# A decoder kernel's attention with heads of eight: heads regrouped by 32 rows, scores issued two units at a time, values once per step

## The chip, the cores and the metric

The kernel runs as one program on 1 core of one Trainium2 chip. The metric is the device time of that core in microseconds (us). The engines are named as the profile names them: PE (TensorE), PEld (its weight loads), DVE (VectorE), ACT (ScalarE), POOL (GpSimd), SP (SyncE). A matrix product reads its stationary operand (the "weights") and its moving operand from SBUF and writes one of eight PSUM banks.

## The reference

Sixteen sequences of 128 tokens, 128 wide, pass through a decoder of four blocks. Each block is self attention, cross attention to a context and a feed-forward part, each followed by a residual sum and a layer norm. What matters here are the five attention layers with 16 heads of 8 columns each:

```python
Q = q_in @ Wq + bq                     # (b, 128, 128) -> 16 heads of 8
scores = einsum('bhqd,bhkd->bhqk', Q, K) / sqrt(8)
scores = causal or windowed or no mask; L1_attn adds a relative bias
attn = softmax(scores)                 # over 128 keys
out = einsum('bhqk,bhkd->bhqd', attn, V) -> (b, 128, 128) @ Wo (+ bo)
```

They are L0_xattn (causal, `h8`), L1_attn (relative bias in windows of 64, `h8p`), L1_xattn (no mask, `h8`), L2_attn and L3_attn (causal, with rotary turning of queries and keys, `h8r`). All values are float32, except the causal mask, which is added by a bfloat16 product.

## The kernel before

`run_loop` is called twice: loop A holds eight layers (L0_attn to L2_xattn, without L2_ffn), loop C the last three. Each runs two iterations over 8 of the 16 sequences. A **step** is one layer on one sequence; a step is split into **units** (`UNITS`): an attention layer with heads of eight has 4 units of 4 heads. So there are 4 layers x 8 sequences x 2 iterations = 64 such steps in loop A and 16 in loop C, 80 steps or 320 units in all. All units of a loop stand in one list, and `plan.slots()` counts through it. In slot n each engine issues, in an order that is written in the code and the same for every slot:

- PE: `scores(n + 3)` (L768), `second(n)` (L821: four 128x128 transposes of the probabilities into the one `second_bank`), `values(n - 1)` (L854), then output and turn of a finished step (L892, L901) and projections of later steps (`project`, L705).
- DVE: `front(n + 3)` (L1154: the negated row maximum; in L1_attn first the bias is added, L1169), `inverse(n + 2)` (L1191), `back(n)` (L1198: copy of `second_bank` to `probs_t`), then residual and statistics (L1233), `normalise` (L1257), and takes of projections (`take`, L1082).
- ACT: `turned(n)` (L1021: the same copy, for the units in `PT_ACT`: unit 3 in `h8`, 2 in `h8p`, 1 and 3 in `h8r`), `outs(n - 1)` (L1034, L1036), `front(n + 3)` (L997, L995: exponentials of 4 heads with their sums), then takes.
- POOL: `probabilities(n + 2)` (L1358: times the inverse sums), and `spread(s)` (L1336) once per step.

Every engine works through its list strictly in order; semaphores hold it where an input is late. There are three score banks; `scores(n)` waits until the unit that used its bank three units earlier has been read (`exp_done`, or `moved` in L1_attn).

How 4 heads share one product: unit i takes heads i, i+4, i+8, i+12. POOL spreads the queries into `Qg`, where copy i holds only rows with (row mod 32) div 8 = i, scaled. The keys stand in `Km` as a block-diagonal matrix, 128 rows by 4 x 128 columns, whose block j holds rows 32j to 32j+31. One product of 128 rows gives the unit's four heads:

```python
mm = pe.matmul(bank[:, :], Qg[:, ring, i, :], Km[:, ring, :, :])            # L803, 128x512
for j in range(4):                                                          # L878, each unit
    mm = pe.matmul(value_bank[32*j:32*j+32, 0:S], Vm[:, ring, i, 32*j:32*j+32],
                   pt[:, j*S:(j+1)*S], start=i == 0, stop=i == 3)
```

`Km`'s blocks are written by four 32-row instructions, on ACT in `h8` and `h8p` (L946), on DVE in `h8r` (L1126). In the trace each float32 product is two MATMUL records (one in transposes and bfloat16 products).

## Time and profile before

| | us |
|---|---|
| median of 3 runs | 2144.5 |
| lowest and highest run | 2141.21, 2146.36 |
| span of the profiled execution | 2139.6 |
| PE busy in it | 1891.7 (88%) |
| DVE busy | 1520.1 (71%) |
| ACT busy | 1370.0 (64%) |
| POOL busy | 827.2 (39%) |

The profiled execution is recorded by its span alone, first to last instruction; no other time is kept for it. The busy shares are averages over stages with different limits, so they say little of any one layer. The two costliest PE lines that the change touches are L803 with 267.6 us in loop A and 67.7 us in loop C, and L878 with 111.1 and 27.7 us.

### The profile page before, as it was taken

The page shows a single profiled execution, that of the slowest core. Times are in us where ns is not written, and L with a number is a line of the kernel's source. Part 1 is how long each engine was busy: PE and PEld are TensorE (multiplying, and loading weights), DVE is VectorE, ACT ScalarE, POOL GpSimd, SP SyncE. Part 2 cuts the span into 40 slices and gives each one's busy share as a digit, 9 for nine tenths or more (in the row PEclk, how much of TensorE's full clock was granted, in tenths as well). Part 3 has the DMA queues.
Part 4 walks back from the last instruction along what each step waited for, and adds up shares of the span by engine and source line. Part 5 has one row for each costly group of instructions (what it writes and reads, how often), then busy time and mean ns, then how long its engine had stood idle before and what let it go on. Part 6 is the DMA issues. An engine that isn't in the chain of part 4 may idle for free. (4 is left out here: it accounts for less than half of the span.)

```text
span 2139.6 us, 40133 instructions
## 1 busy us (share of the span) xinstructions
PE 1891.7 (88%) x13875; PEld 1361.0 (64%) x13945; DVE 1520.1 (71%) x4153; ACT 1370.0 (64%) x5428; POOL 827.2 (39%) x951
## 2 busy tenths in 40 slices
PE   6998989889998998998888999615899996899998
PEld 5757944535786965874444688404467775467776
DVE  4676788788655666779789855695876664786665
ACT  3686589827654587668963765343677774567666
POOL 2461056615432354025643533111543333543334
PEclk9999999979999999999998999867999998999999
DMA  5000000000001000000000000300000000000000
GB/s 228 1 1 1 2 1 1 1 1 2 1 2 34 1 2 1 1 2 1 1 1 1 1 2 1 111 0 13 1 2 1 1 1 24 1 1 1 1 1 11
DMA packets 6980, 24.79 MB, mean 12 GB/s; under 512 B 752, under 2 KB 3440, under 8 KB 6128
## 3 DMA queue, kind: packets, MB, share of 16 engines
q1 hardware_dynamic: 6768, 22.09, 2.8%
q8 instruction: 117, 1.92, 0.4%
q14 instruction: 95, 0.78, 0.1%
HBM read 21.04 MB, written 1.05 MB: 10 GB/s over the span
## 5 line engine op out<-in xcount | busy, mean ns | idle before, releaser
L1358 POOL TENSOR_TENSOR a_probs<-a_probs,a_rinv 128x512 f32<-128x512 f32 x352 | 367.3, 1044 | 421.9 <-DVE a_rinv L1191 417.5
L997 ACT ACTIVATE a_probs<-score_bank,a_negmax 128x128 f32<-128x128 f32 x896 | 315.7, 370 | 64.5 <-DVE a_negmax L1171 62.8
L1358 POOL TENSOR_TENSOR c_probs<-c_probs,c_rinv 128x512 f32<-128x512 f32 x192 | 201.1, 1047 | 296.2 <-DVE c_rinv L1191 294.2
L836 PEld LDWEIGHTS second_bank<-const,a_probs 128*128 128x128 f32 x1408 | 167.4, 142 | 193.4 <-DVE a_probs_t L1198 101.4
L803 PE MATMUL score_bank<-a_km,a_qg 128*128 128x512 f32 x512 | 267.6, 604 | 2.6 <-issue 0.9
L836 PE MATMUL second_bank<-const,a_probs 128*128 128x128 f32 x1408 | 218.4, 278 | 40.8 <-DVE a_probs_t L1198 32.8
L1366 POOL TENSOR_TENSOR a_rstd<-a_ve,neg_half 128x1 f32<-128x1 f32 x128 | 70.5, 551 | 357.6 <-DVE a_ve L1249 356.2
L1171 DVE TENSOR_REDUCE a_negmax<-score_bank 128x4 f32<-128x512 f32 x224 | 154.0, 687 | 67.7 <-PE score_bank L803 53.0
L997 ACT ACTIVATION_READ_ACCUMULATOR a_probs<-score_bank,a_negmax 128x1 f32 x896 | 188.2, 210 | 0.0
L1198 DVE COPY a_probs_t<-second_bank 128x512 f32<-128x512 f32 x272 | 179.6, 660 | 3.9 <-PE second_bank L836 3.9
L1021 ACT ACTIVATE c_probs_t<-second_bank 128x512 f32<-128x512 f32 x160 | 95.3, 595 | 109.9 <-PE second_bank L836 109.5
L995 ACT ACTIVATE c_probs<-c_probs,c_negmax 128x256 f32<-128x256 f32 x256 | 128.0, 500 | 21.4 <-DVE c_negmax L1171 9.5
L836 PEld LDWEIGHTS second_bank<-const,c_probs 128*128 128x128 f32 x768 | 95.2, 142 | 71.9 <-DVE c_probs_t L1198 31.5
L814 PE MATMUL score_bank<-a_xt,w_L_ffn 128*128 128x128 f32 x1024 | 138.8, 279 | 0.0
L836 PE MATMUL second_bank<-const,c_probs 128*128 128x128 f32 x768 | 117.3, 276 | 22.1 <-DVE c_probs_t L1198 19.5
L809 PE MATMUL score_bank<-c_kv,c_q 128*128 128x256 f32 x512 | 133.9, 384 | 0.0
L814 PEld LDWEIGHTS score_bank<-a_xt,w_L_ffn 128*128 128x128 f32 x1024 | 126.1, 194 | 2.7 <-issue 0.6
L1005 ACT ACTIVATE a_hs<-score_bank,w_L_ffn 128x128 f32<-128x128 f32 x256 | 78.4, 364 | 74.8 <-PE score_bank L814 73.5
L997 ACT ACTIVATE c_probs<-score_bank,c_negmax 128x128 f32<-128x128 f32 x256 | 90.5, 377 | 49.2 <-DVE c_negmax L1171 48.3
L1182 DVE SCALAR_TENSOR_TENSOR a_h<-score_bank,w_L_ffn,a_hs 128x128 f32<-128x128 f32 x256 | 77.7, 345 | 57.8 <-ACT a_hs L1005 57.8
L1169 DVE TENSOR_TENSOR c_probs<-score_bank,c_key_mask 128x512 f32<-128x512 f32 x128 | 88.3, 690 | 41.3 <-PE score_bank L809 41.2
L878 PE MATMUL value_bank<-a_probs_t,a_vm 128*32 128x128 f32 x2048 | 111.1, 290 | 0.0
(308 smaller groups left out, 4590.3 us busy)
## 6 DMA issues: line engine op xcount, KB each, us to landing
w_L_ffn<-in_L_ffn SPq DMA_DIRECT2D x1, 3184.0 KB, 14.4
w_L_xattn<-in_L_xattn SPq DMA_DIRECT2D x1, 2112.0 KB, 24.2
w_L_xattn<-in_L_xattn SPq DMA_DIRECT2D x1, 2050.0 KB, 10.3
a_xt<-in_xT SPq DMA_DIRECT2D x3, 512.0 KB, 3.6
a_x<-in_x SPq DMA_DIRECT2D x3, 512.0 KB, 3.7
a_ct<-in_ctxT SPq DMA_DIRECT2D x3, 512.0 KB, 5.8
w_L_attn<-in_L_attn SPq DMA_DIRECT2D x1, 1345.5 KB, 17.2
w_L_attn<-in_L_attn SPq DMA_DIRECT2D x1, 1157.0 KB, 5.8
```

The lines of the kernel that those rows point to most:

```text
L803: mm = pe.matmul(bank[:, :], Qg[:, plan.ring(s, 2), i, :], Km[:, plan.ring(s, 2), :, :].rearrange("p j k -> p (j k)"), start=mask != "caus ...
L809: mm = pe.matmul(bank[:, j * 256:(j + 1) * 256], Q64[:, plan.ring(s, 2), 2 * i + j, :], KV[:, b, :, :].rearrange("p a k -> p (a k)"), star ...
L814: mm = pe.matmul(bank[:, j * S:(j + 1) * S], W(s, "gate_w" if j < 2 else "up_w")[:, c:c + P], XT[:, b, :], start=True, stop=True)
L836: mm = pe.transpose(bank[:, j * S:(j + 1) * S], Pb[:, n % 4, j * S:(j + 1) * S], ident)
L878: mm = pe.matmul(value_bank[32 * j:32 * j + 32, 0:S], Vm[:, plan.ring(s, 2), i, 32 * j:32 * j + 32], pt[:, j * S:(j + 1) * S], start=i == ...
L995: op = act.activation(p, p, ACT.Exp, bias=negmax[:, n % 4, j:j + 1], accum_out=rsum[:, n % 4, j:j + 1])
L997: op = act.activation(p, score_bank[n % 3][:, j * width:(j + 1) * width], ACT.Exp, bias=negmax[:, n % 4, j:j + 1], accum_out=rsum[:, n % 4 ...
L1021: act.activation(PT[:, n % 2, :], second_of(n)[:, :], ACT.Copy).then_inc(sems["pt_act"], 1)
L1169: dve.tensor_tensor(of, heads_view(bank[:, :], heads), add, ALU.add).then_inc(sems["moved"], 1)
L1171: dve.tensor_reduce(negmax[:, n % 4, 0:heads], of, axis=AX.X, op=ALU.max, negate=True).then_inc(sems["negmax_ready"], 1)
L1198: dve.tensor_copy(PT[:, n % 2, :], second_of(n)[:, :]).then_inc(sems["pt_dve"], 1)
L1358: pool.tensor_tensor(p, p, along(rinv[:, n % 4, 0:heads], 512 // heads), ALU.mult).then_inc(sems["norm_done"], 1)
```

## The change

Unit i now takes heads 4i to 4i+3, which are rows 32i to 32i+31 of queries and keys. POOL spreads the keys instead of the queries: copy e in `Kz` holds the keys with only rows of (row mod 32) div 8 = e. A unit's scores are one product of 32 rows (stationary: queries of its 32 rows; moving: `Kz` of these rows, 512 columns). Two units of different rows are issued together at even i, into two banks, so both banks must be free at that time. `Km` is gone, and with it the four 32-row writes; ACT (or DVE) writes queries and keys whole. The values products of all four units stand together after unit 3; so `probs_t` has a ring of 5. To make room for this ring, `Q8`, `K64` and `V64` of loop A share one tensor. The relative bias of L1_attn is read in another order of its columns.

```diff
+PT_RING = 5
@@ Plan.count
+        if stage == "values":
+            return sum(self.kind(s) in SOFTMAX and (self.kind(s) not in H8 or i == 3) for s, i in self.units[:n + 1])
@@ run_loop
-            PT = sb(tag + "probs_t", [P, 2, 512], scope=scope)
+            PT = sb(tag + "probs_t", [P, PT_RING, 512], scope=scope)
-            Qg = sb(tag + "qg", [P, 2, 4, S], scope=scope)
-            Km = sb(tag + "km", [P, 2, 4, S], scope=scope)
+            Kz = sb(tag + "kz", [P, 2, 4, S], scope=scope)
...
-                @block.vector
-                def _(dve):
-                    dve.memset(Km[:, :, :, :], 0.0)
@@ scores(n)
-                        if kind == "lin":
+                        if kind == "lin" or kind in H8 and i % 2:
                             return
...
+                        if kind in H8:
+
+                            two = (n, n + 1)
+                            score_bank_free(n + 1)
+                            if mask == "causal":
+                                for m in two:
+                                    pe.matmul(score_bank[m % 3][:, :], ident_b[:, :], causal_b[:, :, :].rearrange("p a k -> p (a k)"), start=True, stop=False)
+                            for m in two:
+                                group = slice(32 * (i + m - n), 32 * (i + m - n) + 32)
+                                pe.matmul(score_bank[m % 3][:, :], QK[group, plan.ring(s, 2), 0, :], Kz[group, plan.ring(s, 2), :, :].rearrange("p j k -> p (j k)"),
+                                          start=mask != "causal", stop=True).then_inc(sems["scores_ready"], 1)
+                            return
...
-                        elif kind in H8:
-                            mm = pe.matmul(bank[:, :], Qg[:, plan.ring(s, 2), i, :], Km[:, plan.ring(s, 2), :, :].rearrange("p j k -> p (j k)"), start=mask != "causal", stop=True)
@@ values(n)
+                        if kind in H8:
+
+                            if i < 3:
+                                return
+                            for m in range(n - 3, n):
+                                wait_once(pe, sems[plan.copier(m)], plan.count(plan.copier(m), m))
...
-                            for j in range(4):
-                                mm = pe.matmul(value_bank[32 * j:32 * j + 32, 0:S], Vm[:, plan.ring(s, 2), i, 32 * j:32 * j + 32], pt[:, j * S:(j + 1) * S], start=i == 0, stop=i == 3)
+                            for e in range(4):
+                                for j in range(4):
+                                    mm = pe.matmul(value_bank[32 * j:32 * j + 32, 0:S], Vm[:, plan.ring(s, 2), e, 32 * j:32 * j + 32],
+                                                   PT[:, (n - 3 + j) % PT_RING, e * S:(e + 1) * S], start=e == 0, stop=e == 3)
@@ scalar: take
-                            for j in range(4):
-                                rows = slice(32 * j, 32 * j + 32)
-                                op = act.activation(Km[rows, plan.ring(s, 2), j, :], bank[rows, S:2 * S], ACT.Identity, bias=W(s, "bk")[rows, :])
+                            op = act.activation(QK[:, plan.ring(s, 2), 1, :], bank[:, S:2 * S], ACT.Identity, bias=W(s, "bk"))
@@ vector: take
-                            for j in range(4):
-                                rows = slice(32 * j, 32 * j + 32)
-                                dve.tensor_tensor(Km[rows, plan.ring(s, 2), j, :], QK[rows, plan.ring(s, 2), 1, :], RT2[rows, plan.ring(s, 2), 1, :], ALU.add)
-                            dve.tensor_tensor(QK[:, plan.ring(s, 2), 0, :], QK[:, plan.ring(s, 2), 0, :], RT2[:, plan.ring(s, 2), 0, :], ALU.add).then_inc(sems["rope_ready"], 1)
+                            dve.tensor_tensor(QK[:, plan.ring(s, 2), :, :], QK[:, plan.ring(s, 2), :, :], RT2[:, plan.ring(s, 2), :, :], ALU.add).then_inc(sems["rope_ready"], 1)
@@ gpsimd: spread
-                        pool.tensor_tensor(Qg[:, plan.ring(s, 2), :, :], over(QK[:, plan.ring(s, 2), 0, :], 4), along(head_scale, S), ALU.mult).then_inc(sems["masked"], 1)
+                        pool.tensor_tensor(Kz[:, plan.ring(s, 2), :, :], over(QK[:, plan.ring(s, 2), 1, :], 4), along(head_scale, S), ALU.mult).then_inc(sems["masked"], 1)
```

How PE's list moves, at one step of L2_attn. First the kernel before, from the scores of the next step's unit 0 (L798 is the causal mask, L803 the scores, L836 the transposes, L878 the values, L898 the output of the step that ended before):

```order
L798 MATMUL score_bank0<-causal_b,ident_b 128x512 [waits body_masked,body_exp_done]
L803 MATMUL score_bank0<-a_km,a_qg 128x512
L836 MATMUL second_bank<-const,a_probs 128x128 [waits body_norm_done,body_pt_dve]
L836 MATMUL second_bank<-const,a_probs 128x128 x3
L878 MATMUL value_bank<-a_probs_t,a_vm 32x128 [waits body_out_taken]
L878 MATMUL value_bank<-a_probs_t,a_vm 32x128 x3
L798 MATMUL score_bank1<-causal_b,ident_b 128x512 [waits body_exp_done]
L803 MATMUL score_bank1<-a_km,a_qg 128x512
L836 MATMUL second_bank<-const,a_probs 128x128 [waits body_norm_done,body_pt_act]
L836 MATMUL second_bank<-const,a_probs 128x128 x3
L878 MATMUL value_bank<-a_probs_t,a_vm 32x128 x4
L898 MATMUL proj_bank1<-w_L2_attn,a_ot 128x128 [waits body_proj_by_dve]
```

The same stretch in the changed kernel (L808 is the mask, L811 the scores, L851 the transposes, L921 the output):

```order
L808 MATMUL score_bank0<-causal_b,ident_b 128x512 [waits body_exp_done,body_masked]
L808 MATMUL score_bank1<-causal_b,ident_b 128x512
L811 MATMUL score_bank0<-a_kz,a_qk 128x512
L811 MATMUL score_bank1<-a_kz,a_qk 128x512
L851 MATMUL second_bank<-const,a_probs 128x128 [waits body_norm_done,body_pt_dve]
L851 MATMUL second_bank<-const,a_probs 128x128 x3
L851 MATMUL second_bank<-const,a_probs 128x128 [waits body_norm_done,body_pt_act]
L851 MATMUL second_bank<-const,a_probs 128x128 x3
L921 MATMUL proj_bank1<-w_L2_attn,a_ot 128x128 [waits body_out_taken,body_proj_by_dve]
```

Before, a unit's scores stand ahead of every group of transposes, and values behind it. Now the scores of two units stand together, and two groups of transposes of one bank follow each other directly. The second half of the same step, where the values (L900) stand:

```order
L808 MATMUL score_bank2<-causal_b,ident_b 128x512 [waits body_exp_done]
L808 MATMUL score_bank0<-causal_b,ident_b 128x512
L811 MATMUL score_bank2<-a_kz,a_qk 128x512
L811 MATMUL score_bank0<-a_kz,a_qk 128x512
L851 MATMUL second_bank<-const,a_probs 128x128 [waits body_norm_done,body_pt_dve]
L851 MATMUL second_bank<-const,a_probs 128x128 x3
L851 MATMUL second_bank<-const,a_probs 128x128 [waits body_norm_done,body_pt_act]
L851 MATMUL second_bank<-const,a_probs 128x128 x3
L900 MATMUL value_bank<-a_probs_t,a_vm 32x128 x16
L731 MATMUL proj_bank2<-w_L2_attn,a_xt 128x128 [waits body_proj_by_dve]
```

Again two groups of transposes stand side by side; all sixteen values products of the step come behind the second, ahead of the projections of later steps.

DVE's list where it turns queries and keys in L2_attn, before (L1126 writes the key blocks, L1127 the queries):

```order
L1096 TENSOR_TENSOR a_qk<-proj_bank,w_L_attn 128x256 [waits body_proj_ready]
L1097 TENSOR_TENSOR a_rt<-proj_bank,w_L_attn 128x256
L1126 TENSOR_TENSOR a_km<-a_qk,a_rt 32x128 [waits body_proj_by_dve]
L1126 TENSOR_TENSOR a_km<-a_qk,a_rt 32x128 x3
L1127 TENSOR_TENSOR a_qk<-a_qk,a_rt 128x128
L1171 TENSOR_REDUCE a_negmax<-score_bank 128x4 [waits body_scores_ready]
```

and now, with one instruction (L1145) in place of five:

```order
L1117 TENSOR_TENSOR a_qk<-proj_bank,w_L_attn 128x256 [waits body_proj_ready]
L1118 TENSOR_TENSOR a_rt<-proj_bank,w_L_attn 128x256
L1145 TENSOR_TENSOR a_qk<-a_qk,a_rt 128x256 [waits body_proj_by_dve]
L1189 TENSOR_REDUCE a_negmax<-score_bank 128x4 [waits body_scores_ready]
```

## Rows read from the trace of the kernel before

**Rows 1.** The page's first line.
```profile
span 2139.6 us, 40133 instructions
```

**Rows 2.** Stretch, us; busy (count) of PE, PEld, DVE, ACT, POOL; PEclk; DMA.
```profile
280.00:344.00 64.00, 56.01 (x401) 27.95 (x399) 58.41 (x131) 57.43 (x252) 38.29 (x44) 1.00 0.01 1
360.00:425.00 65.00, 57.91 (x441) 32.78 (x437) 50.76 (x132) 57.39 (x276) 40.85 (x47) 1.00 0.01 1
490.00:550.00 60.00, 58.96 (x447) 35.78 (x452) 49.10 (x132) 48.45 (x230) 35.36 (x38) 1.00 0.01 2
```

**Rows 3.** DVE L1099, once per step: first and last start in five stretches.
```profile
L1099 DVE TENSOR_TENSOR a_vm<-proj_bank,const x7: 674/681/682, 97.2 to 155.3; 128x512 f32<-128x512 f32 x7
...
L1099 DVE TENSOR_TENSOR a_vm<-proj_bank,const x7: 679/680/681, 282.3 to 343.7; 128x512 f32<-128x512 f32 x7
...
L1099 DVE TENSOR_TENSOR a_vm<-proj_bank,const x7: 673/675/681, 363.0 to 420.6; 128x512 f32<-128x512 f32 x7
...
L1099 DVE TENSOR_TENSOR a_vm<-proj_bank,const x6: 674/681/692, 494.9 to 543.4; 128x512 f32<-128x512 f32 x6
...
L1099 DVE TENSOR_TENSOR c_vm<-proj_bank,const x4: 678/678/678, 1523.9 to 1554.7; 128x512 f32<-128x512 f32 x4
```

**Rows 4.** Timeline of PE, one step of L2_attn: start us, length us, engine, line.
```profile
515.24 1.02 PE L803 MATMUL score_bank<-a_km,a_qg 128*128 128x512 f32 x2
516.10 0.60 PE L836 MATMUL second_bank<-const,a_probs 128*128 128x128 f32 x4
516.63 0.43 PE L878 MATMUL value_bank<-a_probs_t,a_vm 128*32 128x128 f32 x8
516.99 0.39 PE L798 MATMUL score_bank<-causal_b,ident_b 128*128 128x512 bf16 x1
517.22 1.02 PE L803 MATMUL score_bank<-a_km,a_qg 128*128 128x512 f32 x2
...
518.96 0.49 PE L898 MATMUL proj_bank<-w_L_attn,a_ot 128*128 128x128 f32 x2
519.29 0.38 PE L798 MATMUL score_bank<-causal_b,ident_b 128*128 128x512 bf16 x1
...
523.80 0.39 PE L724 MATMUL proj_bank<-a_xt,w_L_attn 128*128 128x128 f32 x2
...
524.69 0.27 PE L910 MATMUL proj_bank<-const,a_x 128*128 128x128 f32 x1
525.02 1.02 PE L803 MATMUL score_bank<-a_km,a_qg 128*128 128x512 f32 x2
```

**Rows 5.** Timeline of PE in L1_xattn: scores directly behind values.
```profile
388.34 1.12 PE L803 MATMUL score_bank<-a_km,a_qg 128*128 128x512 f32 x2
389.30 0.60 PE L836 MATMUL second_bank<-const,a_probs 128*128 128x128 f32 x4
```

**Rows 6.** Timeline of DVE, PE, ACT in L2_attn: copies and exponentials.
```profile
519.84 0.66 DVE L1198 COPY a_probs_t<-second_bank 128x512 f32<-128x512 f32 x1
...
520.56 0.42 PEld L836 LDWEIGHTS second_bank<-const,a_probs 128*128 128x128 f32 x4 [0.86 <-DVE a_probs_t L1198]
...
521.25 0.60 ACT L1021 ACTIVATE a_probs_t<-second_bank 128x512 f32<-128x512 f32 x1
...
522.07 0.37 ACT L997 ACTIVATE a_probs<-score_bank,a_negmax 128x128 f32<-128x128 f32 x1 [0.22 <-DVE a_negmax L1171]
...
523.61 0.28 ACT L1036 ACTIVATE a_ot<-value_bank 128x128 f32<-128x128 f32 x1
```

**Rows 7.** Timeline of DVE in L2_attn: turned keys, then the next row maximum.
```profile
516.10 1.17 DVE L1126 TENSOR_TENSOR a_km<-a_qk,a_rt 32x128 f32<-32x128 f32 x4
...
517.49 0.68 DVE L1171 TENSOR_REDUCE a_negmax<-score_bank 128x4 f32<-128x512 f32 x1
```

**Rows 8.** Timeline of ACT in L1_xattn: keys spread to blocks, between two units' exponentials.
```profile
382.32 1.46 ACT L946 ACTIVATE a_km<-proj_bank,w_L_xattn 32x128 f32<-32x128 f32 x4
...
384.11 0.37 ACT L997 ACTIVATE a_probs<-score_bank,a_negmax 128x128 f32<-128x128 f32 x1
```

More of the change, by code:

```diff
@@ L542, in run_loop @@
             RT2 = sb(tag + "rt", [P, 2, 2, S], scope=scope)
-            Qg = sb(tag + "qg", [P, 2, 4, S], scope=scope)
-            Km = sb(tag + "km", [P, 2, 4, S], scope=scope)
+            Kz = sb(tag + "kz", [P, 2, 4, S], scope=scope)
             Vm = sb(tag + "vm", [P, 2, 4, D], scope=scope)
             nkeys = 2 * S if last_loop else S
-            V64 = sb(tag + "v64", [P, 2, nkeys // S, 1024], scope=scope)
             H = sb(tag + "h", [P, 4, 2, S], scope=scope)
@@ L550, in run_loop @@
             if last_loop:
+                V64 = sb(tag + "v64", [P, 2, nkeys // S, 1024], scope=scope)
                 Q64 = sb(tag + "q64", [P, 2, 16, S], scope=scope)
@@ L562, in run_loop @@
                 Qz = sb(tag + "qz", [P, 2, 8, 2, S], scope=scope)
-                K64 = sb(tag + "k64", [P, 2, 8, S], scope=scope)
+                ends = sb(tag + "ends", [P, 4096], scope=scope)
+                K64 = ends[:, 0:2048].rearrange("p (a c k) -> p a c k", a=2, c=8)
+                V64 = ends[:, 2048:4096].rearrange("p (a o d) -> p a o d", a=2, o=1)
                 CT = sb(tag + "ct", [P, G, S], scope=scope)
-                Q8 = sb(tag + "q8", [P, 3, 8, S], scope=scope)
+                Q8 = ends[:, 0:3072].rearrange("p (a h k) -> p a h k", a=3, h=8)
                 K8 = sb(tag + "k8", [P, 3, S], scope=scope)
@@ L766, in project, with score_bank_free @@
                         mm.then_inc(sems["proj_ready"], 1)
-                    def scores(n):
-                        s, i, kind, b = plan.unit(n)
-                        if kind == "lin":
-                            return
-                        bank = score_bank[n % 3]
+                    def score_bank_free(n):
                         last = [k for k in range(n) if k % 3 == n % 3 and plan.unit(k)[2] in STAGES["scores"]]
@@ L779, in scores @@
                             wait_once(pe, sems[done[0]], plan.count(done[1], last[-1]))
+                    def scores(n):
+                        s, i, kind, b = plan.unit(n)
+                        if kind == "lin" or kind in H8 and i % 2:
+                            return
+                        bank = score_bank[n % 3]
+                        score_bank_free(n)
                         if i == 0:
@@ L863, in values @@
                                     after_reader(pe, s, name)
+                        if kind in H8:
+                            if i < 3:
+                                return
+                            for m in range(n - 3, n):
+                                wait_once(pe, sems[plan.copier(m)], plan.count(plan.copier(m), m))
                         wait_once(pe, sems[stage], plan.count(stage, n))
@@ L871, in values @@
                             wait_once(pe, sems["acc_done"], plan.count("acc", experts[-1]))
-                        pt = PT[:, n % 2, :]
+                        pt = PT[:, n % PT_RING, :]
                         if kind == "mqa":
@@ L1020, in turned @@
                             m = plan.count("second", n) - 1
-                            act.activation(PT[:, n % 2, :], second_of(n)[:, :], ACT.Copy).then_inc(sems["pt_act"], 1)
+                            act.activation(PT[:, n % PT_RING, :], second_of(n)[:, :], ACT.Copy).then_inc(sems["pt_act"], 1)
                     def outs(n):
@@ L1164, in front @@
                                 if kind == "h8p":
-                                    add = heads_view(W(s, "relpos")[:, i * 512:(i + 1) * 512], heads)
+                                    add = W(s, "relpos").rearrange("p (e u k) -> p u e k", e=4, u=4)[:, i, :, :]
                                 else:
@@ L1197, in back @@
                             dve.wait_ge(sems["second_ready"], m + 1)
-                            dve.tensor_copy(PT[:, n % 2, :], second_of(n)[:, :]).then_inc(sems["pt_dve"], 1)
+                            dve.tensor_copy(PT[:, n % PT_RING, :], second_of(n)[:, :]).then_inc(sems["pt_dve"], 1)
                         elif kind in STAGES["acc"]:
```

## The prediction

> **What bounds the kernel now.** The page gives one span of 2139.6 us [rows 1] and shares of busy time that mix all layers, so I went from there to the stretches, one per layer that the change touches, then to the number of steps in each, then to the order of events inside one step.
>
> The stretches [rows 2] are L1_attn (280:344), L1_xattn (360:425) and L2_attn (490:550). The reader is to see that another engine is nearly full in each. In L1_attn it is DVE, 58.41 of 64 us (91%). In L1_xattn DVE, ACT and PE are busy 50.76, 57.39 and 57.91 of 65. In L2_attn it is PE, 58.96 of 60 (98%). The granted clock is 1.00 in all three.
>
> The length of a step comes from an instruction that runs once per step [rows 3]: L0_xattn (155.3 - 97.2) / 6 = 9.68 us, L1_attn 61.4 / 6 = 10.23, L1_xattn 57.6 / 6 = 9.60, L2_attn 48.5 / 5 = 9.70, L3_attn 30.8 / 3 = 10.27. Each stands for 16 steps of the program.
>
> PE's timeline of one L2_attn step [rows 4] gives the cost of each piece, from one start to the next: causal mask 0.23, scores of a unit 0.86, four transposes 0.53, values 0.36, output 0.33, the four query and key projections 0.89, one transpose of the state 0.11 (the rest of its 0.33 is the next mask). With v at 0.33 the sum is 4 x 1.98 + 0.33 + 0.33 + 0.89 + 0.11 = 9.58, against 9.70 measured. So PE waits almost nowhere in this layer: scores cover the copy of each group of transposes. In the same rows eight values records of 32 columns take 0.43 us together, so narrow products in different parts of the array do run beside each other.
>
> **The change, part by part.**
>
> *Scores.* Two units' scores are products of 32 rows in different row groups. If they run together as the values do, a pair costs 0.86 in place of 1.72: PE saves 2 x 0.86 = 1.72 us per step, 138 us over 80 steps. No row shows products side by side by rows. The bounds are 0.86 (together) and 1.72 (one after the other). I take 0.86, since the values are the nearest row.
>
> *Changes between wide and narrow products.* A scores product right behind the values takes 1.12 in place of 1.02, and the transposes start 0.96 later in place of 0.86 [rows 5]: 0.10 for the exposed load. I take 0.20 for entering a narrow pair (the same again for the emptying) and 0.10 for leaving; the bounds are 0 and 0.4 per pair. The Trainium skill (TensorEngine Tiling (Array Packing), Key Properties) says that changing the tiling mode drains TensorE, which speaks against the change. What it costs goes by the rows: before there are 8 changes per step, now 6 (in and out of two pairs and of one block of values), so the count is no loss.
>
> *Values.* The same 16 products; as one block they need 4 x 0.26 = 1.05 and 0.10 once. But all 1.15 us now stand behind the last copy of the step and ahead of the projections, where before only the last 0.36 did.
>
> *Order.* This is the part that costs. In the new list T(1), T(2) (transposes of units 1 and 2) are neighbours, and so are T(3), T(0'), where ' is the next step. There is one `second_bank`, so the second group waits for the copy C of the first. A group ends 0.60 after its start, a copy takes 0.60 to 0.66, and the next transposes follow 0.06 later [rows 4, 6]; PE needs 0.43 for the group itself, so it stands for some 0.85 us, twice per step, with nothing to do. And the pair of units 2', 3' needs the bank of unit 0', so PE waits for an exponential that follows the pair before it: scores, maximum 0.68 [rows 7], four exponentials 1.54 (522.07 to 523.61) [rows 6].
>
> The step of L2_attn worked out, with 0 at the mask of pair (0', 1'): masks 0.45, change 0.20, scores ready 0.45 + 0.20 + 1.02 = 1.67, PE free at 1.6. T(1) 1.6 to 2.0, ended 2.2. ACT copies it to 2.8. T(2) 2.9 to 3.3, output to 3.75. The maximum of 0' ends at 2.4, its exponentials stand behind ACT's copy: 2.75 to 4.25. Pair (2', 3') starts at 4.4; PE free 6.0. T(3) to 6.4, ended 6.6, ACT's copy 7.2. T(0') 7.3 to 7.75. Values 7.85 to 9.0, v 9.33, queries and keys 10.22, state and start of the next pair 10.45. So 10.45 against 9.70: +0.75.
>
> The other layers by the same list:
> - L0_xattn: copy of unit 1 is on DVE behind the maximum, T(2) at 3.15; pair (2', 3') at 4.05; only two projections (0.45). The next pair starts at 9.65: 0.0.
> - L1_xattn: no masks, so scores are ready at 1.12 and pair (2', 3') starts at 3.55, T(0') at 5.95, next pair at 8.6. Here ACT also loses the block writes: 1.46 us (L946) [rows 8] become one of about 0.25. -1.0.
> - L1_attn: no mask either, and both maxima and bias sums on DVE. DVE holds C(3) back to 7.55, then T(0'), values and projections bring the next pair to 10.35. +0.1.
> - L3_attn: as L2_attn, 10.35 to 10.45, since DVE turns keys in one instruction of about 0.41 in place of 1.17 + 0.21 up to the next maximum [rows 7]. Before, that delayed the maximum. +0.1.
>
> Sum: 16 x (0.0 - 1.0 + 0.1 + 0.75 + 0.1) = -1 us. My schedule leaves out small slips: for L2_attn before it gave 9.58 where 9.70 was measured. I add 0.15 per step, 12 us. Total +11.
>
> *Free edits.* The cleared `Km` and the shared tensor cost no time on a path; POOL's spread is the same 128x512 product. If these were wrong it would be by less than 1 us each. DMA is untouched.
>
> The profiled execution then has a span of 2139.6 + 11 = 2151; the median of the runs, 2144.5, lies 4.9 above the old span, so I predict 2156 us.
>
> **The rivals.**
>
> *A: the waits are absorbed (faster).* The engines are queues, and a wait of 0.85 us on PE costs nothing if another engine is behind anyway. Then a step falls to the largest sum of work. For PE in L2_attn that is 2 x (0.45 + 0.2 + 0.86 + 0.1) + 4 x 0.43 + 1.25 + 0.33 + 0.33 + 0.89 + 0.11 = 7.85; ACT and DVE stand near the same. With 0.8 on top, L0_xattn, L2_attn and L3_attn give about 1.1 per step, 48 x 1.1 = 53, L1_xattn 16, L1_attn (DVE, 91% full) 3: 2156 - 12 - 72 = 2072 us. It decides if copies of a group start before PE has run out of other work. For it: PE is the fullest engine in three layers and loses 1.7 us of work. Against it: the list has nothing between the neighbours but an output of 0.33 in one gap. Chance 0.22.
>
> *B: the pair does not run side by side.* Then each pair costs 0.86 more, on the path in every layer: 160 x 0.86 = 138, 2156 + 138 = 2294. For it: no row shows it. Against it: the values. The Trainium skill (TensorE: Matmul & The Clock Gate, Part 3) reports 3.07 times for four row tiles of 512 columns. By that rule the sum stays the forecast's 2156; no run here shows it yet. Chance 0.11.
>
> *C: the clock falls in L1_attn.* The granted clock is 1.00 there now [rows 2], with PE at 88%; PE's work per step falls to some 6 of 10.3 us. At half the clock (1.2 in place of 2.4 GHz) these 6 us double; if that befalls a quarter of 16 steps, it is 24 us: 2180. The Trainium skill (TensorE: Matmul & The Clock Gate, Part 1) makes the lower clock the state of a little-used array. Chance 0.05.
>
> **How the numbers follow.** The forecast has 0.62. Its own range is 0.4 us per step either way, 32 us, about 2125 to 2188. A measurement of this kernel can tell about 0.2% (4.3 us) from no change. Of the forecast's 0.62, 0.09 lie below 2140 and 0.14 within 2140 to 2149; with A that is faster 0.31, same 0.14, and slower 0.55 with B and C. The range leaves out B and about half of A: 2095 to 2200.
>
> **What would show it.** Right: scores of the two units start within a few ns of each other; PE waits for copies (L836's line) about 0.6 to 0.8 us twice per step where it waited almost never; L2_attn's step is near 10.5 us and L1_xattn's near 8.7; PE busy falls by over 100 us while the span does not. Wrong: a step of L2_attn near 8.7 (A), a pair's scores over 1.7 us (B), a clock below 1.00 in L1_attn (C). It is also wrong if L1_xattn does not gain, since then ACT was not what held it.

## The result and the profile after

| | before | changed |
|---|---|---|
| median, us (9 runs each) | 2144.61 | 2153.0 |
| lowest to highest | 2140.53 to 2147.58 | 2145.83 to 2158.89 |
| span of the profiled execution | 2139.6 | 2144.2 |

The ratio is 1.0039 with a 95% interval of 1.0024 to 1.0054: slower by 0.4%. The profiled execution (2145.83 us) is the fastest of the nine. The mean granted clock of the whole program is 0.923 to 0.933 in the nine executions; in the runs of the kernel before that were taken beside the experiments it is 0.955 to 0.961.

The first line of the profile's page and its line of engine totals:
```profile
span 2144.2 us, 40009 instructions
...
PE 1806.9 (84%) x13885; PEld 1330.1 (62%) x13945; DVE 1481.6 (69%) x4023; ACT 1307.3 (61%) x5284; POOL 825.5 (38%) x951
```
PE's busy time fell by 85 us, ACT's by 63, and the span grew by 4.6. Where that went stands in the page's costliest groups:
```profile
L851 PE MATMUL second_bank<-const,a_probs 128*128 128x128 f32 x1408 | 240.5, 296 | 115.6 <-DVE a_probs_t L1216 77.3
...
L811 PE MATMUL score_bank<-a_kz,a_qk 32*128 32x512 f32 x512 | 156.7, 689 | 1.5
```
Both groups are those of loop A. Its scores cost 156.7 us where L803 cost 267.6. PE's idle time in front of the transposes (L836 before, L851 now) is 115.6 us; before it was this:
```profile
L836 PE MATMUL second_bank<-const,a_probs 128*128 128x128 f32 x1408 | 218.4, 278 | 40.8 <-DVE a_probs_t L1198 32.8
```
So in loop A 111 us of products went and 75 us of waiting came, most of it for copies.

The stretches that answer to [rows 2], and one that holds L1_attn of the second iteration:
```profile
280.00:344.00 64.00, 43.47 (x355) 26.24 (x355) 57.13 (x130) 48.93 (x231) 37.74 (x44) 0.92 0.00 1
360.00:415.00 55.00, 45.90 (x429) 28.02 (x431) 47.47 (x120) 48.40 (x248) 39.93 (x46) 1.00 0.01 2
490.00:550.00 60.00, 49.06 (x437) 30.30 (x443) 40.06 (x107) 43.43 (x211) 32.15 (x35) 1.00 0.00 1
947.00:1041.00 94.00, 76.10 (x447) 45.91 (x446) 66.33 (x145) 54.40 (x252) 42.52 (x49) 0.59 0.00 1
```
The kernel before, in the last of these:
```profile
947.00:1041.00 94.00, 82.00 (x575) 42.06 (x575) 82.66 (x189) 84.28 (x366) 54.28 (x63) 1.00 0.01 1
```
No engine is over 90% busy in the first three, and in the fourth the granted clock is 0.59 where it was 1.00: most of the time PE runs at 1.2 in place of 2.4 GHz.

The instruction once per step, as [rows 3] (L1099 is now L1120), and once more for that second L1_attn:
```profile
L1120 DVE TENSOR_TENSOR a_vm<-proj_bank,const x7: 682/692/692, 96.7 to 154.7; 128x512 f32<-128x512 f32 x7
...
L1120 DVE TENSOR_TENSOR a_vm<-proj_bank,const x7: 677/680/691, 283.9 to 346.6; 128x512 f32<-128x512 f32 x7
...
L1120 DVE TENSOR_TENSOR a_vm<-proj_bank,const x8: 671/674/692, 356.7 to 416.1; 128x512 f32<-128x512 f32 x8
...
L1120 DVE TENSOR_TENSOR a_vm<-proj_bank,const x5: 691/691/692, 496.4 to 537.5; 128x512 f32<-128x512 f32 x5
...
L1120 DVE TENSOR_TENSOR a_vm<-proj_bank,const x7: 691/692/692, 958.7 to 1041.1; 128x512 f32<-128x512 f32 x7
...
L1120 DVE TENSOR_TENSOR c_vm<-proj_bank,const x4: 678/678/691, 1530.2 to 1561.4; 128x512 f32<-128x512 f32 x4
```

Each figure is a mean from the first to the last start in its stretch; the first steps of a stage differ from those that repeat later.

| us per step | before | forecast | after |
|---|---|---|---|
| L0_xattn | 9.68 | 9.7 | 9.67 |
| L1_attn, iteration 1 | 10.23 | 10.3 | 10.45 (10.15 in its last four) |
| L1_attn, iteration 2 | 10.2 | 10.3 | 13.7 |
| L1_xattn | 9.60 | 8.6 | 8.49 |
| L2_attn | 9.70 | 10.45 | 10.28 |
| L3_attn | 10.27 | 10.4 | 10.4 |

The same step of L2_attn as [rows 4], in PE's timeline:
```profile
517.64 0.27 PE L933 MATMUL proj_bank<-const,a_x 128*128 128x128 f32 x1
517.97 0.38 PE L808 MATMUL score_bank<-causal_b,ident_b 128*128 128x512 bf16 x1
518.28 1.13 PE L811 MATMUL score_bank<-a_kz,a_qk 32*128 32x512 f32 x4
519.34 0.66 PE L851 MATMUL second_bank<-const,a_probs 128*128 128x128 f32 x4
520.68 0.66 PE L851 MATMUL second_bank<-const,a_probs 128*128 128x128 f32 x4 [0.69 <-ACT a_probs_t L1042]
521.17 0.39 PE L921 MATMUL proj_bank<-w_L_attn,a_ot 128*128 128x128 f32 x2
522.17 0.59 PE L808 MATMUL score_bank<-causal_b,ident_b 128*128 128x512 bf16 x2 [0.61 <-ACT a_probs L1018]
522.69 1.13 PE L811 MATMUL score_bank<-a_kz,a_qk 32*128 32x512 f32 x4
523.75 0.65 PE L851 MATMUL second_bank<-const,a_probs 128*128 128x128 f32 x4
525.09 0.66 PE L851 MATMUL second_bank<-const,a_probs 128*128 128x128 f32 x4 [0.69 <-ACT a_probs_t L1042]
525.68 0.53 PE L900 MATMUL value_bank<-a_probs_t,a_vm 128*32 128x128 f32 x12
```
A pair of units' scores takes 1.06 us from start to next start (518.28 to 519.34). The first of the two masks has no record of its own; it starts 0.11 behind the transpose of the state, at 517.75. The group of four transposes of unit i is T(i), as in the prediction. With 0 at the first mask, T(1) is at 1.6, T(2) at 2.9, pair (2', 3') with its masks at 4.4, T(3) at 6.0, T(0') at 7.3 and the values at 7.9. The prediction's schedule had 1.6, 2.9, 4.4, 6.0, 7.3 and 7.85.

### The profile page after: what moved, and what is told of

Same layout as the page of the kernel before. It is cut to its first block and busy times, and to the rows that moved or that the text cites. A ratio compares the mean times of both kernels' runs of the same rounds, so it can differ in the third digit from the quotient of the medians.

```text
span 2144.2 us, 40009 instructions
## 1 busy us (share of the span) xinstructions
PE 1806.9 (84%) x13885; PEld 1330.1 (62%) x13945; DVE 1481.6 (69%) x4023; ACT 1307.3 (61%) x5284; POOL 825.5 (38%) x951
## 3 DMA queue, kind: packets, MB, share of 16 engines
HBM read 21.04 MB, written 1.05 MB: 10 GB/s over the span
## 5 line engine op out<-in xcount | busy, mean ns | idle before, releaser
L851 PE MATMUL second_bank<-const,a_probs 128*128 128x128 f32 x1408 | 240.5, 296 | 115.6 <-DVE a_probs_t L1216 77.3
L851 PEld LDWEIGHTS second_bank<-const,a_probs 128*128 128x128 f32 x1408 | 162.2, 148 | 250.6 <-DVE a_probs_t L1216 107.6
L811 PE MATMUL score_bank<-a_kz,a_qk 32*128 32x512 f32 x512 | 156.7, 689 | 1.5
L851 PE MATMUL second_bank<-const,c_probs 128*128 128x128 f32 x768 | 121.3, 282 | 29.7 <-ACT c_probs_t L1042 17.5
L851 PEld LDWEIGHTS second_bank<-const,c_probs 128*128 128x128 f32 x768 | 92.8, 143 | 75.4 <-ACT c_probs_t L1042 24.6
L1016 ACT ACTIVATE a_probs<-a_probs,a_negmax 128x128 f32<-128x128 f32 x256 | 99.3, 390 | 37.3 <-DVE a_negmax L1189 37.3
```

Source lines behind the costliest of these rows:

```text
L811: pe.matmul(score_bank[m % 3][:, :], QK[group, plan.ring(s, 2), 0, :], Kz[group, plan.ring(s, 2), :, :].rearrange("p j k -> p (j k)"), sta ...
L851: mm = pe.transpose(bank[:, j * S:(j + 1) * S], Pb[:, n % 4, j * S:(j + 1) * S], ident)
L1016: op = act.activation(p, p, ACT.Exp, bias=negmax[:, n % 4, j:j + 1], accum_out=rsum[:, n % 4, j:j + 1])
```

## The experiments

Theory 1: the pairing works, and the new order eats its gain in waits for the copies (one `second_bank`) and for the exponential of unit 0' (three score banks). Theory 2: the fall of the clock in L1_attn turns what is left of the gain into a loss. Each ratio is to runs of the kernel before that were taken beside it (medians 2143.4 to 2143.6). Steps and clocks are those of the one profiled execution of each kernel.

### One unit at a time
```diff
-                        if kind == "lin" or kind in H8 and i % 2:
+                        if kind == "lin":
...
-                            two = (n, n + 1)
-                            score_bank_free(n + 1)
+                            two = (n,)
```


> The 32-row scores stay, but one unit is issued per slot, so that on TensorE scores and transposes alternate again and no pair runs side by side. Theory 1 (the new order with its waits for the copies through one second bank, and the wait for an exponential, eats what the pairing saves): TensorE gets up to 1.7 us of work per step back but loses two idle stretches of 0.85 us, so a step of L2_attn is between 9.6 and 10.3 us (10.26 with the change), L1_xattn stays between 8.6 and 9.2, and with the clock at 1.00 in L1_attn of the second iteration (13.6 us per step with the change) the total is 2110 to 2135. Rival A (the waits are absorbed, the pairing is a clean gain): removing it makes every step longer by 0.9 us or more, total 2200 or more. Rival D (what costs is the values as one block, or the other regrouping, not the order): L2_attn stays at 10.2 or more, total near 2150.

Measured: 2175.87 us, ratio 1.0147 (1.0121 to 1.0174). PE's timeline in L2_attn:
```profile
515.17 0.38 PE L807 MATMUL score_bank<-causal_b,ident_b 128*128 128x512 bf16 x1
515.48 1.12 PE L810 MATMUL score_bank<-a_kz,a_qk 32*128 32x512 f32 x2
516.53 0.66 PE L850 MATMUL second_bank<-const,a_probs 128*128 128x128 f32 x4
```
One 32-row unit alone takes 1.05 us (515.48 to 516.53), a pair 1.06: the two run side by side all but completely. It is 0.19 more than the 0.86 of the 128-row product [rows 4], and the mask ahead takes 0.31 where it took 0.23. The step of L2_attn is 10.07, in the expected 9.6 to 10.3; its waits are gone, and PE is busy 57.3 of 59 us (486 to 545). But L1_xattn is at 9.21 in place of 8.50 and L0_xattn at 9.62 in place of 9.46. The clock in L1_attn is 0.81 and 0.88, and in L3_attn of the second iteration it fell too, with two steps of 13.2 and 17.6 us in place of 11.6 and 9.8. So the total missed the expected 2110 to 2135 by 40 us, in part by the steps and in part by the clock. Issued singly, 32-row products gain 0.19 per step in L2_attn and 0.08 in L3_attn, and cost in L0_xattn and L1_xattn, where the pairing is worth more than its waits. And the clock fell in L1_attn although PE was busy 93% and 91% of these stretches (a share that the lower clock itself raises):
```profile
278.00:368.00 90.00, 83.50 (x477) 43.20 (x475) 72.66 (x160) 61.72 (x284) 45.52 (x52) 0.81 0.00 1
969.00:1054.00 85.00, 77.25 (x477) 40.37 (x478) 72.45 (x160) 61.99 (x284) 45.44 (x52) 0.88 0.00 1
```

### Transposes in two banks
```diff
-                return value_bank if kind in ("moe", "lin", "ffn") and i % 2 else second_bank
+                return value_bank if kind in ("moe", "lin", "ffn") + H8 and i % 2 else second_bank
```


> Everything of the change stays; the transposes of units 1 and 3 go into value_bank in place of second_bank, so that two neighbouring groups of transposes no longer share a bank. Theory 1: the two idle stretches of some 0.85 us per step in front of the second group go; the wait for the exponential stays. L2_attn falls from 10.26 to 8.9 to 9.6 us per step, the idle time in front of the transposes (115.6 us in all with the change) falls to under 60, total 2080 to 2125 (the lower end if the clock holds in L1_attn). Rival D (the wait for the exponential or the block of values sets the step, the copy waits only lie beside it): L2_attn stays within 0.2 of 10.26 and the total within 10 us of 2150.

Measured: 2114.09 us, ratio 0.986 (0.9835 to 0.9885), 39 us below the changed kernel. The page's group of transposes and PE's waits in 490 to 550:
```profile
L851 PE MATMUL second_bank<-const,a_probs 128*128 128x128 f32 x896 | 146.7, 290 | 20.2 <-POOL a_probs L1376 17.7
```
```profile
PE score_bank L808 <- ACT a_probs L1018: 7.6, 5, 1.5
PE value_bank L900 <- ACT a_probs_t L1042: 1.0, 4, 0.3
```
The same view of the changed kernel:
```profile
PE second_bank L851 <- ACT a_probs_t L1042: 7.6, 11, 0.7
PE score_bank L808 <- ACT a_probs L1018: 3.0, 5, 0.6
```
The group above is that of `second_bank` alone; the other 512 transposes are in `value_bank` now. The waits for copies ended, as theory 1 says. Of the 1.4 us per step that they took in L2_attn, 0.9 came back as a longer wait for the exponential (0.6 to 1.5), so a step at full clock is 9.68, 0.6 shorter and 0.08 above the expected 8.9 to 9.6. Few steps of L2_attn reached that in this execution: the clock fell briefly there too, and from the first to the last of eight starts the two iterations took 73.7 and 71.8 us, where the changed kernel took 71.4 twice. The gain of the total is elsewhere: L0_xattn fell from 9.46 to 8.87, L1_xattn from 8.50 to 7.92. The clock was lost in both L1_attn this time (0.69 and 0.74), with steps up to 12.23 us; in that layer waits for POOL and for the copy ahead of the values came in place of those for `second_bank`'s copy. A part of the 39 us is the clock's: the second L1_attn took 17 us less than in the changed kernel, the first 7 more.

### Filling L1_attn with overwritten mask products
```diff
+                            if kind == "h8p":
+                                for m in two:
+                                    pe.matmul(score_bank[m % 3][:, :], ident_b[:, :], causal_b[:, :, :].rearrange("p a k -> p (a k)"), start=True, stop=True)
```


> Everything of the change stays; in L1_attn alone each pair of scores is preceded by two bf16 products of 128x512 whose result the scores overwrite, the same products that the masked layers have there. Theory 2 (TensorE with too little work in L1_attn loses the clock, and that makes a small gain a small loss): steps of L1_attn in the second iteration fall from 13.6 us to 10.2 to 10.8, the granted clock between about 940 and 1040 us goes from 0.63 to over 0.9, the total falls by 15 to 30 us to 2123 to 2138, and the runs lie closer together. Rival E (the clock fall has another cause, as where in the program it stands): the clock stays near 0.63 there and the total rises by 0 to 10 us. Rival F (it moves elsewhere): L1_attn is cured, another stretch of the trace shows a low clock, total unchanged.

Measured: 2154.51 us (2149.33 to 2157.63). The clock of L1_attn rose to 0.90 in the second iteration but fell to 0.79 in the first, where the changed kernel had 0.94, and steps were 10.8 to 15 us. Theory 2's number failed: four bf16 mask products per step do not hold the clock. One iteration gained what the other lost and the total stayed, which is near to rival F. The run tells nothing against theory 2 itself, as the clock was not restored.

With both edits at once:

> Both edits together: transposes of units 1 and 3 in value_bank, and two overwritten products before each pair in L1_attn. Theory 1 and theory 2 together: the gains add, 2065 to 2110, under both kernels. If theory 2 is wrong, it equals the run with two banks within 8 us; if theory 1 is wrong, it equals the run with the filled L1_attn within 8 us.

Measured: 2111.39 us (2099.05 to 2124.6), ratio 0.9855 (0.9798 to 0.9913). That is as with the two banks alone, the branch in which the fill does nothing, but with four runs 25 us apart a gain of some us could not be told. In the profiled execution the clock of L1_attn was higher, 0.86 and 0.91 (285 to 345 and 945 to 1038) against 0.67 and 0.71 without the fill, and each L1_attn only 3 to 4 us shorter.

### Wide against narrow fill
Ahead of each pair in L1_attn, overwritten by it, once
```diff
+                                pe.matmul(bank[:, :], QK[:, plan.ring(s, 2), 0, :], Kz[:, plan.ring(s, 2), :, :].rearrange("p j k -> p (j k)"), start=True, stop=True)
```
and once the pair's own two 32-row products a second time.

> The change, and in L1_attn alone one float32 product of 128 rows and 512 columns ahead of each pair, overwritten by it: some 0.86 us of TensorE per pair, twice per step. Its partner in this call puts the same time of 32-row products there. Theory 2a (the clock in L1_attn is lost because wide float32 work was taken away, the kind of work matters): the granted clock in both iterations of L1_attn is over 0.95, its steps are 10.2 to 11.3 us (13.6 in the second iteration with the change), the total 2125 to 2145. Theory 2b (only TensorE's busy time matters): clock and steps equal to the partner's. Rival E (neither, the clock falls in this place whatever TensorE does): clock below 0.9 in at least one of the two iterations, total 2150 to 2180.

> The change, and in L1_attn alone each pair of 32-row products is issued twice, the second time overwriting the first: about 1.06 us more of TensorE per pair, but no wide product. Theory 2a: the clock in L1_attn still falls, to 0.6 to 0.9 in at least one iteration, and since the added work then also runs at the lower clock the total is 2150 to 2185, 15 us or more above the partner with wide products. Theory 2b: the clock stays near 1.00 as with the partner, total 2125 to 2150. Rival E: as 2a here, but then the partner loses the clock too.

Measured: 2167.88 us with wide products (1.0111, 1.0082 to 1.014), 2194.12 with narrow ones (1.0239, 1.0179 to 1.0299). Both are above what theory 2a expected, 2125 to 2145 and 2150 to 2185. Both L1_attn stages, with wide products:
```profile
276.00:372.00 96.00, 73.00 (x509) 41.16 (x508) 72.65 (x160) 61.64 (x285) 45.48 (x52) 0.91 0.00 1
962.00:1058.00 96.00, 72.99 (x509) 41.08 (x507) 72.65 (x160) 61.69 (x284) 45.48 (x52) 0.91 0.00 1
```
and with narrow ones:
```profile
277.00:391.00 114.00, 95.14 (x541) 52.66 (x538) 73.55 (x162) 61.65 (x284) 46.61 (x54) 0.66 0.00 1
980.00:1094.00 114.00, 95.13 (x541) 52.59 (x537) 73.69 (x162) 61.76 (x284) 46.50 (x53) 0.66 0.00 1
```
Theory 2b (busy time alone decides) falls: about the same added time (0.86 and 1.06 us per pair at full clock) gave a clock of 0.91 or of 0.66, the higher one where PE was busy for less of the stretch, and the runs are 26 us apart. Theory 2a is right in its direction, not in its size: one wide product per pair does not give 1.00 back, and standing on PE's path it costs a step of 12.6 to 13.1 us even so. The total alone would also fit rival E; the run with L1_attn as before, below, rules that out.

### Keys written by four activations
```diff
-                            op = act.activation(QK[:, plan.ring(s, 2), 1, :], bank[:, S:2 * S], ACT.Identity, bias=W(s, "bk"))
+                            for j in range(4):
+                                rows = slice(32 * j, 32 * j + 32)
+                                op = act.activation(QK[rows, plan.ring(s, 2), 1, :], bank[rows, S:2 * S], ACT.Identity, bias=W(s, "bk")[rows, :])
```


> The change, with one part undone in size: the keys of h8 and h8p layers are again written by four activations of 32 rows in place of one of 128. My prediction put the whole gain of L1_xattn (9.6 to 8.5 us per step) on this relief of ScalarE. If so, L1_xattn goes back to 9.2 to 9.7 us, L0_xattn and L1_attn by 0 to 0.6, L2_attn stays at 10.26, and the total rises by 10 to 30 us to 2163 to 2183. Rival H (L1_xattn gained by the pairing on TensorE, not by ScalarE): L1_xattn stays within 0.2 of 8.50 and the total within 5 us of 2153.

Measured: 2211.09 us, ratio 1.0335 (1.0302 to 1.0368). The timeline of ACT, first here in L0_xattn, then in L1_xattn of the changed kernel:
```profile
108.71 1.46 ACT L969 ACTIVATE a_qk<-proj_bank,w_L_xattn 32x128 f32<-32x128 f32 x4
```
```profile
383.57 0.39 ACT L967 ACTIVATE a_qk<-proj_bank,w_L_xattn 128x128 f32<-128x128 f32 x1
```
L1_xattn's steps are 9.3 to 9.5 us where the clock was full and up to 12.4 where it was not, L0_xattn's 9.99 in place of 9.46, L2_attn's 10.26 as before. So the relief of ScalarE carries some 0.8 to 1.0 us per step of L1_xattn, as the prediction had it, and rival H falls. The total is 28 us above what was expected, and there the clock comes in again: L1_attn is at 0.61 and 0.68, and the clock fell in parts of L0_xattn and L1_xattn too.

### L1_attn alone as before
The 32-row form stays in `h8` and `h8r`; `h8p` gets `Qg`, `Km` and their lines back, of which the two on PE are these:
```diff
-                        if kind in H8:
+                        if kind in ("h8", "h8r"):
...
+                        elif kind == "h8p":
+                            mm = pe.matmul(bank[:, :], Qg[:, plan.ring(s, 2), i, :], Km[:, plan.ring(s, 2), :, :].rearrange("p j k -> p (j k)"), start=True, stop=True)
```


> The change in every layer but L1_attn, which goes back to the old form: block-diagonal keys, one product of 128 rows per unit, values after each unit. In the traces so far the 16 steps of L1_attn take 162 us before and 185 us with the change, though a step at full clock is 10.33 and 10.15 us. Theory 2 (the clock loss in L1_attn is what makes the change slower): L1_attn takes 160 to 165 us in all at a clock of 1.00, the rest stays, total 2122 to 2138, below the kernel before, and the runs within 6 us. Rival E (the clock falls at this place in any regrouped kernel): clock below 0.95 in L1_attn, total 2143 or more. Rival F (it moves to the neighbours L1_xattn or L2_attn): L1_attn cured, one of them longer by 10 us or more, total 2143 or more.

Measured: 2129.33 us (2127.2 to 2133.89), ratio 0.9939 (0.9926 to 0.9953). Both stages of L1_attn:
```profile
276.00:356.00 80.00, 69.60 (x489) 35.66 (x488) 72.36 (x162) 71.08 (x307) 45.74 (x52) 1.00 0.00 1
945.00:1025.00 80.00, 69.62 (x488) 35.52 (x486) 72.37 (x163) 70.93 (x307) 45.76 (x52) 1.00 0.01 1
```
This is the test of theory 2, and it holds: clock 1.00, steps of 10.34, the other layers unchanged (L0_xattn 9.46, L1_xattn 8.50, L2_attn 10.26, L3_attn 10.15), the total in the middle of the expected range, its runs 7 us apart for the expected 6. The edit takes back the whole regrouping of L1_attn, its waits included. But at full clock the regrouped L1_attn was no slower: its steps repeat at 10.15 in the first iteration of the changed kernel. So what the edit gives back is the clock. With the regrouping in L1_attn the kernel is slower than before by 8 us, without it faster by 14.

### The version that beats both
The same with two banks in the regrouped layers, and that with another copying engine (`"h8r": (1, 3)` to `"h8r": (2,)`):

> The same, with the transposes of units 1 and 3 in value_bank in the layers that are still regrouped. Theories 1 and 2 together: the 2114 us of the two banks less the 13 us that its L1_attn takes over 162, and less what the lower clock cost behind it: 2090 to 2108, the fastest so far. If the clock then falls in L0_xattn, L1_xattn or L2_attn instead, 2108 to 2125.

> The kernel of the run before in this call, and in L2_attn and L3_attn ScalarE copies the transposed probabilities of unit 2 alone and VectorE those of 0, 1 and 3, where ScalarE had 1 and 3. With two banks TensorE waits 1.5 us per step of L2_attn for the exponential of unit 0', which stands on ScalarE behind the copy of unit 1. If that copy is what delays it: the wait falls by 0.2 to 0.6 us, L2_attn from 9.68 to 9.1 to 9.5 per step, total 5 to 15 us below its partner. If VectorE is then the one that is late (its maximum and its copies stand in one queue): steps the same or longer, total 0 to 15 us above.

Measured: 2097.65 us, ratio 0.9787 (0.9767 to 0.9806), and 2096.2 us, ratio 0.9799 (0.9772 to 0.9826). These are the fastest kernels of this study, 46 and 47 us below before. With L1_attn wide and its clock at 1.00 in both, the two banks for transposes alone are worth 32 us (2129.3 to 2097.7). The kernel with the other copying engine does not differ from its partner in total: L2_attn fell to 9.48 per step (9.67 with its partner), the wait for the exponential from 1.5 to 1.2 us, but L3_attn rose from 9.68 to 10.28. There ScalarE waited for VectorE's maximum, where its partner shows no such wait in the same stretch (1490 to 1513); that is the second branch of the expectation:
```profile
ACT c_probs L1035 <- DVE c_negmax L1206: 6.4, 7, 2.1
```

### A fourth bank for scores
```diff
-N_PROJ = 3
+N_PROJ = 2
...
-        score_bank = [ctx.enter_context(nc.psum_tensor(f"score_bank{i}", [P, 512], F32)) for i in range(3)]
+        score_bank = [ctx.enter_context(nc.psum_tensor(f"score_bank{i}", [P, 512], F32)) for i in range(4)]
```


> The kernel with transposes in two banks (2114 us), and besides a fourth bank for scores, taken from the three of the projections. There the pair of units 2 and 3 waited 1.5 us per step in L2_attn for the exponential of unit 0, since three banks don't hold two pairs. Theory 1 (both waits are what the pairing turned into, and each is a matter of a bank): the wait in front of the pair's mask is gone, L2_attn falls from 9.68 to 8.2 to 9.0 us per step, L0_xattn from 8.87 to under 8.6, and the total is 2040 to 2105, the upper end where two projection banks cost something in other stages. Rival D (another engine sets the step by now, the wait lies beside it): L2_attn stays above 9.4 and the total within 15 us of 2114. Rival G (two projection banks cost more than the fourth score bank gives): L2_attn shorter, the other stages longer, total above 2125.

Measured: 2177.42 us, ratio 1.0165 (1.0144 to 1.0186). PE's waits in 510 to 555, a stretch of L2_attn:
```profile
PE proj_bank L933 <- DVE a_vm L1120: 4.1, 4, 1.1
PE second_bank L851 <- POOL a_probs L1376: 3.1, 4, 0.8
```
The wait of the pair's mask is gone, and one for a projection bank, 1.1 us per step, stands in its place; L2_attn is at 9.95. The kernel has the two banks for transposes too, so it is to be held against that one's 2114. It is rival G, and worse than its text: L1_xattn rose from 7.92 to 8.9 to 9.2, L0_xattn from 8.87 to 9.4, and the mean clock of the whole program is 0.911 to 0.918 where it was 0.922 to 0.927. Only L3_attn gained (9.68 to 9.2). So where the wait for the exponential leads to can't be read from this run alone; no run gave the pair a fourth bank without taking it from somebody.

## Why the prediction was right, and where it was not

The number (2156 against 2153.0) and the direction are right; the sum behind them is not. Two errors of about 24 us cancel, and that is luck. The kernel that leaves L1_attn alone is at 2129.3, so in the other four layers the change is worth about -14 us, not the +11 of the forecast (of which L1_attn had 1.6). The regrouping of L1_attn adds 24 us, by the clock, which stood as rival C with a chance of 0.05.

*Bound now.* Right. PE had been full in L2_attn, and in the changed kernel a repeating step of L2_attn is still as long as PE's list with its three waits. The sign that PE's busy time falls by over 100 us did not quite come: it fell by 85, with products in L1_attn that took longer at the lower clock.

*Scores.* Right. The two units' products start 7 ns apart (at 518.279 and 518.286 us), and a pair takes 1.06 against 1.05 for one unit. Rival B is out: issued singly the same products cost 23 us more in all. The Trainium skill (TensorE: Matmul & The Clock Gate, Part 3) has products on different row tiles of the array run at the same time; the trace agrees, with the 1.06.

*Changes between wide and narrow.* Right in sum: 0.30 per pair taken, 0.20 measured in the pair (1.06 less 0.86) and 0.08 in a mask (0.31 less 0.23). The Trainium skill (TensorEngine Tiling (Array Packing), Key Properties) states that a change of tiling mode drains TensorE. The 0.28 us fit that, but no run here shows a drain as such.

*Order.* Right, to 0.1 us at each point of the step of L2_attn. The waits are real and on the path: taking one kind away gave 39 us, and 32 where the clock of L1_attn held. So rival A (the waits are absorbed, 2072) is out.

*Layers.* Taken from the kernel with L1_attn as before: from the first to the last start of the once-per-step instruction in a stage, seven steps, both iterations summed. L0_xattn +0.1 us (forecast 0), L1_xattn -16 (forecast 14 x -1.0), L3_attn +3 (14 x 0.1), L2_attn +4 where the forecast had 14 x 0.75 = +10.5. L2_attn is the term that was mis-sized. Its steps repeat at 10.26, not 10.45, most of that because the block of values takes 1.01 us (525.68 to 526.69) and not 1.15. And only the last three steps of a stage lose what was forecast, 0.7 each; the first four together lose nothing (the first is 10.96 against 11.43). In all -9 for -2. In L3_attn the granted clock fell as well, from 0.95 and 0.93 (1487 to 1567, 1817 to 1899) to 0.88 in both iterations of the changed kernel, so its +3 may be in part the clock's; no run separates the two.

This kernel can't test the term of L1_attn, as the layer is not regrouped in it. The changed kernel shows it where its clock was full: steps repeat at 10.15 us where they repeated at 10.33 before, so -0.2 where the forecast had +0.1.

*The slip of 0.15 per step, +12 us.* Wrong, and it had no ground. It came from a step of 9.70 where the list gave 9.58. But 9.70 is a mean over five steps that begin with 10.09 and 9.77; the last three of that stage before are 9.55, 9.59 and 9.58, as the list has it. After the change steps of L1_xattn repeat at 8.50 or 8.51 and of L2_attn at 10.26, four times in a row, with no slip. Layers and slip together are 7 + 12 = 19 of the 24 us; the rest lies between the stages, which the sum did not look at.

*The clock (rival C).* The mechanism was right (wide work goes away in L1_attn, then the clock falls), and the chance of 0.05 was far too low. That the size agrees (24 us given, 24 found: 2153.0 less 2129.3) is luck: the rival had a quarter of 16 steps longer by 6 us, and in the profiled execution nearly all eight steps of the second iteration are longer by 3.4 (13.60 against 10.15), those of the first hardly at all. The step that failed is that I read a granted clock of 1.00 as safe. PE was busy 56.01 of 64 us in that stretch of [rows 2]; after the change it is 43.47, the 128-row scores are gone from it, and there is no mask product in that layer. The Trainium skill (TensorE: Matmul & The Clock Gate, Part 1) ties the clock to how busy the array has been. The trace agrees in direction; but the busy share alone doesn't foretell it. Of the two fills, the one with the lower share kept the higher clock, and with one unit at a time PE was busy for more of the stretch than before the change (93% and 91% for 87%) and lost the clock all the same. So the longer waits of the new order are not the whole cause either.

## What to carry to other kernels

Products of 32 rows on different row groups did run side by side here, and then it was the list of banks that decided: whoever issues two producers together needs banks for both their results, so look for neighbours in the new order that share one bank, before counting the saved time. The Trainium skill (TensorEngine Tiling (Array Packing), Restrictions and Gotchas) says that row tiling increases PSUM pressure. The trace agrees for the scores: a pair takes two of three banks, and TensorE waits 0.6 us per step of L2_attn until the bank of unit 0' is read. The 32 to 39 us of `second_bank` come on top, from the order. In a layer where another engine is nearly full, packing TensorE gains little (0.2 us of 10.3 in L1_attn) and can lose its clock (24 us here); try such a layer wide as well. And judge a sum by its parts: here a kernel 46 us faster was hidden behind a number that looked right.

## What was not expected of the hardware

One float32 product of 32 rows and 512 columns alone takes 1.05 us, and two on neighbouring row groups 1.06, where one of 128 rows takes 0.86. The Trainium skill (TensorE: Matmul & The Clock Gate, Why this matters for your kernels) has a single 32-row product at the time of one of 128 rows. Between wide products, as here, the trace differs: it is 0.19 more.

The granted clock followed the kind of work more than its share of time. The stretches of L1_attn, all at the same place of the program: 128-row products, PE busy 87%, 1.00; 32-row products issued singly, busy 93% and 91%, 0.81 and 0.88; 32-row pairs, 0.94 and 0.61 in the two iterations of one execution (why the second fell so much further is open); the pairs doubled, busy 83%, 0.66 twice; the pairs with a wide product ahead, busy 76%, 0.91 twice. What exactly the chip counts no run here shows. The loss seems to make the spread too: the nine runs of the changed kernel lie 13 us apart, those before 7, and the five with L1_attn as before 7.
